# Context and weights laid out by the host with the contraction on partitions, and one tile for the last FFN chunk

## What is computed

```python
q = x @ Wq.T
k_raw = context @ Wk.T
v_raw = context @ Wv.T
kv = jnp.concatenate([k_raw, v_raw], axis=-1)
kv = kv.reshape(b, m, NHEADS, HEAD_DIM, 2)
q = _rmsnorm(q)
k = _rmsnorm(k)
scores = jnp.einsum('bhnd,bhmd->bhnm', q, k) * scale
attn = jax.nn.softmax(scores, axis=-1)
out = jnp.einsum('bhnm,bhmd->bhnd', attn, v)
W = (wq.astype(jnp.float32) - ZERO_POINT) * scale[:, None]
return jnp.einsum('bsd,hd->bsh', x, W)
...
gate = jax.nn.silu(gate)
return _qlinear(gate * up, wq_down, s_down)
...
x = x + jnp.tanh(g_xattn[0]) * _L0_xattn_ref(_layernorm(x, axis=-1), ctx_2048, L0_xattn_Wq, L0_xattn_Wk, L0_xattn_Wv)
x = x + jnp.tanh(g_ffn[0]) * _L0_ffn_ref(_layernorm(x, axis=-1), L0_ffn_wq_gate, L0_ffn_s_gate, L0_ffn_wq_up, L0_ffn_s_up, L0_ffn_wq_down, L0_ffn_s_down)
```

## Time and profile before

| what | us |
|---|---|
| three runs: median (lowest to highest) | 267.28 (266.71 to 267.42) |
| the profiled execution | 267.05 |
| its span in the profile | 265.2 |
| start of turn0 in iterations 2 to 5 | 107.66, 133.47, 159.28, 185.06 |
| one iteration of the loop | 25.8 |

### The profile page before, as it was taken

How to read it: one execution, slowest core, us unless ns; L and a number is a source line. 1 busy time by engine, 2 the same in 40 slices (tenths; PEclk the granted TensorE clock), 3 DMA queues, 4 the chain that set the end, 5 groups by cost and what they waited for, 6 DMA issues and landing times.

```text
span 265.2 us, 7329 instructions
## 1 busy us (share of the span) xinstructions
PE 219.6 (83%) x2592; PEld 178.5 (67%) x2592; DVE 176.5 (67%) x583; ACT 177.8 (67%) x338; POOL 106.3 (40%) x145
## 2 busy tenths in 40 slices
PE   1663979659879999899989989998999697965864
PEld 1553758437657878688777868786878585855764
DVE  4487999934665776687658765876596674657162
ACT  3258585844867895789578867885897667534250
POOL 5012212021322463645464455446444735434451
PEclk9999597956988999999999999999999999996799
DMA  5897522233075022603160406050506070000001
GB/s 178 216 352 178 62 56 49 54 45 62 0 101 101 0 56 49 136 3 72 26 138 0 87 12 138 0 100 3 121 0 82 13 109 2 21 22 0 20 20 40
DMA packets 45127, 18.08 MB, mean 68 GB/s; under 512 B 36400, under 2 KB 44848, under 8 KB 45104
## 3 DMA queue, kind: packets, MB, share of 16 engines
q1 hardware_dynamic: 45104, 17.77, 31.6%
HBM read 7.28 MB, written 2.10 MB: 35 GB/s over the span
## 4 chain that ended last, share of the span: by engine, by line
DVE 30%; PE 29%; issue 15%; POOL 14%; ACT 7%; DMA 2%; SPq 1%; DVEq 1%; POOLq 0%; ACTq 0%
PE bank L1278 7%; PE bank L1363 5%; POOL qk_parts L422 4%; POOL qk_unit L462 4%; PE pv_ps L1242 4%; POOL h_lo L430 4%; PE bank L1388 3%; DVE sums L899 3%; DVE hidden L990 3%; PE score_ps L1223 2%; PE bank L1311 2%; DVE silu L975 2%; DMA w_raw<-L_xattn_Wv_dram 2%; POOL x_all L439 2%; PE bank L1265 2%
## 5 line engine op out<-in xcount | busy, mean ns | idle before, releaser
L526 ACT ACTIVATE probs<-score_ps 128x1024 f32<-128x1024 f32 x64 | 65.9, 1032 | 3.5 <-PE score_ps L1223 3.5
L1363 PE MATMUL bank<-x_hi,gu_hi 128*128 128x256 f32 (+1 forms) x192 | 51.0, 301 | 4.7 <-DVE hidden L990 2.0
L462 POOL TENSOR_TENSOR qk_unit<-qk_raw,root_y 128x512 f32<-128x512 f32 x16 | 17.4, 1085 | 85.4 <-DVE root_y L783 85.4
L1363 PE MATMUL bank<-x_lo,gu_hi 128*128 128x256 f32 (+1 forms) x192 | 48.4, 286 | 0.0
L1242 PE MATMUL pv_ps<-probs,v_blocks 128*32 128x128 f32 x1024 | 42.8, 286 | 6.2 <-issue 4.2
L430 POOL TENSOR_TENSOR h_lo<-hidden,h_hi 128x256 fp32r<-128x256 f32 (+1 forms) x48 | 35.3, 745 | 24.8 <-ACT h_hi L651 24.4
L1363 PEld LDWEIGHTS bank<-x_hi,gu_hi 128*128 128x128 f32 (+1 forms) x192 | 35.3, 184 | 9.5 <-DVE hidden L990 2.4
L1363 PEld LDWEIGHTS bank<-x_lo,gu_hi 128*128 128x128 f32 (+1 forms) x192 | 35.5, 185 | 0.0
L1242 PEld LDWEIGHTS pv_ps<-probs,v_blocks 128*32 128x32 f32 x1024 | 24.9, 112 | 15.5 <-issue 7.4
L640 ACT ACTIVATE tanh_g<-bank,half_gate 128x256 f32<-128x256 f32 (+1 forms) x48 | 22.8, 475 | 18.2 <-PE bank L1363 16.0
L1278 PE MATMUL bank<-w_hi,xc_hi 128*128 128x256 f32 x96 | 31.7, 330 | 2.4 <-DVE xc_lo L889 2.4
(11 more groups left out here) (108 smaller groups left out, 435.2 us busy)
## 6 DMA issues: line engine op xcount, KB each, us to landing
ctx_sb<-ctx_dram SPq DMA_DIRECT2D x16, 128.0 KB, 2.6
out_dram<-x_all SPq DMA_DIRECT2D x16, 128.0 KB, 1.8
x_all<-x_dram SPq DMA_DIRECT2D x1, 1536.0 KB, 10.5
dn_int<-L_ffn_wq_down_dram SPq DMA_DIRECT2D x1, 704.0 KB, 6.7
gu_int<-L_ffn_wq_gate_dram SPq DMA_DIRECT2D x1, 640.0 KB, 4.6
gu_int<-L_ffn_wq_up_dram SPq DMA_DIRECT2D x1, 640.0 KB, 5.7
x_all<-x_dram SPq DMA_DIRECT2D x1, 384.0 KB, 5.1
w_raw<-L_xattn_Wq_dram SPq DMA_DIRECT2D x1, 256.0 KB, 2.7
```

The lines of the kernel that those rows point to most:

```text
L462: nc.gpsimd.tensor_tensor(qk_unit[:], qk_raw[:], root_y[:, 0:2 * H].unsqueeze(2).to_broadcast([P, 2 * H, HD]), ALU.mult).then_inc(unit_rea ...
L526: nc.scalar.activation(probs[:, t % 2, :], score_ps[t % 2][:].rearrange("p h n -> p (h n)"), ACT.Exp, scale=float(HD) ** 0.5 / UNIT ** 2). ...
L1363: last = nc.tensor.matmul(bank[k][0:r, a * TOK:(a + 1) * TOK], w[:, j, a, c, 0:r], xx[:, c, :], start=(n == 1), stop=(n == (4 if wide_weig ...
```

## The change

The host hands over ctx transposed, (tile, 128, 2, 128) with the contraction first; the three W matrices transposed, with their columns already in the order in which the kernel stores heads; the gate and up integers transposed in 6 chunks of 128 rows; and the down integers transposed. In the last gate/up chunk the 64 gate rows and the 64 up rows form one tile of 128; in the last down chunk the 64 rows stand twice.

The kernel loses all transposes of ctx, W and FFN weights, with `prep`. xc_hi and xc_lo are drained from the bank for x alone (128x256). ctx is split straight from SBUF: `context_hi` on ScalarE and `context_lo` on GpSimd. FFN weights are split from the integers by `upper_ffn` (ScalarE, three of 128x1536, p=-1) and `lower_ffn` (VectorE, three of 128x1536, p=0); `widest_weight` now looks for a lower part that is not zero. `normalize` and `normalize2` move from ScalarE to VectorE as one tensor_scalar each, and their offsets go. K is projected before Q. Chunk 5 has 4 matmuls for 8: the gate comes out on partitions 0 to 63, the up half on 64 to 127. h_hi(5) is written to rows 64 to 127 and h_lo(5) to rows 0 to 63 of the same tile, so that down needs 1 matmul there for 2. Four issues of small loads become one, five of FFN weights two.

```diff
+    columns = (order[:, None] * HD + np.arange(HD)).reshape(-1)
+    keys_values = np.concatenate([Wk, Wv])
+    w = np.stack([Wq[columns], keys_values[0::2][columns], keys_values[1::2]])
+    w_t = w.transpose(0, 2, 1).reshape(3, KC, P, D).transpose(0, 2, 1, 3)
+    ctx_t = ctx.transpose(0, 2, 1).reshape(B, KC, P, S).transpose(0, 2, 1, 3)
+    gate_up = np.zeros((NJ, 2, P, D), np.int32)
...
+        gate_up[NJ - 1, 0, a * LAST:(a + 1) * LAST] = w[full:]
...
+    gu_t = gate_up.reshape(NJ, 2, P, KC, P).transpose(4, 0, 1, 3, 2)
...
+    down[NJ - 1, :LAST] = down[NJ - 1, LAST:2 * LAST] = wq_down.T[full:]
...
+            sp.dma_start(ctx_sb[:, 0, :, :], ctx[0]).then_inc(ctx_loaded[0], 16)
+            for m in (1, 0, 2):
+                sp.dma_start(w_raw[:, m, :, :], w_qkv[m]).then_inc(w_loaded[m], 16)
...
-            full = (NJ - 1) * P
-            for k, s in enumerate((s_gate, s_up)):
-                with nc.allow_non_contiguous_dma(reason="704 scales, one to a partition"):
-                    sp.dma_start(scales[:, k, 0:NJ - 1], s[0:full].rearrange("(j p) -> p j", p=P)).then_inc(small_loaded, 16)
-                sp.dma_start(scales[0:LAST, k, NJ - 1:NJ], s[full:HID].rearrange("(p j) -> p j", j=1)).then_inc(small_loaded, 16)
-            for k, w in enumerate((wq_gate, wq_up)):
-                sp.dma_start(gu_int[:, k, 0:NJ - 1, :], w[0:full, :].rearrange("(j p) d -> p j d", p=P)).then_inc(ffn_w_loaded, 16)
-                sp.dma_start(gu_int[0:LAST, k, NJ - 1, :], w[full:HID, :]).then_inc(ffn_w_loaded, 16)
-            sp.dma_start(dn_int[:], wq_down.rearrange("(c p) h -> p c h", p=P)).then_inc(ffn_w_loaded, 16)
+            sp.dma_start(scales[:, 0:2, :], s_gu).then_inc(small_loaded, 16)
+            sp.dma_start(gu_int[:], w_gu).then_inc(ffn_w_loaded, 16)
+            sp.dma_start(dn_int[:], w_dn).then_inc(ffn_w_loaded, 16)
             sp.dma_start(x_all[:, 4:B, :], x[4:B].rearrange("b p d -> p b d")).then_inc(x_loaded[2], 16)
...
-                    sp.wait_ge(ctx_turned, b + 3)
-                    sp.dma_start(ctx_sb[:, e, :], dram_tile(ctx, b + 4)).then_inc(ctx_loaded[e], 16)
+                    sp.wait_ge(ctx_lo_ready, b + 3)
+                    sp.dma_start(ctx_sb[:, e, :, :], ctx[b + 4]).then_inc(ctx_loaded[e], 16)
...
+                of = hidden_rows(j)
+                lower = h_lo[:, j, :] if j < NJ - 1 else h_hi[0:LAST, j, :]
+                if j == NJ - 1:
+                    pool.wait_ge(h_lo_ready, n)
+                nc.gpsimd.tensor_tensor(lower, hidden[of, j % 3, :], h_hi[of, j, :].bitcast(F32),
                                         ALU.subtract).then_inc(h_lo_ready, 1)
+                if j == NJ - 1:
+                    pool.wait_ge(h_lo_ready, n + 1)
+
+            def context_lo(p, e):
+
+                b = 2 * p + e
+                if has_tile(p, b + 2):
+                    pool.wait_ge(ctx_hi_ready, b + 3)
+                    nc.gpsimd.tensor_tensor(xc_lo[:, e, KC:2 * KC, :], ctx_sb[:, e, :, :], xc_hi[:, e, KC:2 * KC, :].bitcast(F32),
+                                            ALU.subtract).then_inc(ctx_lo_ready, 1)
 
             def add_attention(p, e):
...
                 split_chunks(p - 1, 1, (0, 1))
+                context_lo(p, 1)
                 qk_norm(p, 0)
                 split_chunks(p, 2, (2,))
                 split_qk(p, 0)
                 split_chunks(p, 2, (3, 4, 5))
                 add_attention(p, 1)
+                context_lo(p + 1, 0)
                 qk_norm(p, 1)
                 split_qk(p, 1)
-                if real(p, "y0"):
+                if here(p, "y0"):
...
+            def upper_ffn(part):
 
 ...
+                act.wait_ge(ffn_w_loaded, 16 * 2)
+                nc.scalar.activation(ffn_part(part, gu_hi, dn_hi), ffn_part(part, gu_int, dn_int), ACT.Identity,
+                                     bias=minus_zero_point[:]).then_inc(ffn_hi_ready, 1)
...
+                    nc.scalar.copy(xc_hi[:, e, 0:KC, :].rearrange("p a n -> p (a n)"), bank[k][:, 0:D]).then_inc(xc_hi_ready, 1)
+
+            def context_hi(p, e):
+
+                b = 2 * p + e
+                if has_tile(p, b + 2):
+                    act.wait_ge(ctx_loaded[e], 16 * (p + 2))
+                    if since(b, 0):
+                        k, m = use(p, "v0") if e else use(p - 1, "v1")
+                        act.wait_ge(filled[k], m)
+                    nc.scalar.copy(xc_hi[:, e, KC:2 * KC, :], ctx_sb[:, e, :, :]).then_inc(ctx_hi_ready, 1)
...
                 drain_v(p, 0)
-                if not first:
-                    normalize(p, 0)
+                context_hi(p, 1)
...
                 exp_octet(p, 1, 1)
                 if not ending(p):
                     upper(p, 2, 3)
-                    normalize2(p, 0)
                 upper(p, 2, 4)
                 drain_v(p, 1)
+                context_hi(p + 1, 0)
                 upper(p, 2, 5)
                 if first:
-                    convert_gate_up()
+                    upper_ffn(0)
                     square(p, 1)
                     copy_qk(p, 1)
-                    convert_down()
-                    normalize(p, 1)
+                    upper_ffn(1)
+                    upper_ffn(2)
                 else:
-                    normalize(p, 1)
                     square(p, 1)
                     copy_qk(p, 1)
...
+                nc.vector.tensor_scalar(xn[:, 1 - e, :], tile_of(b), x_mean_var[:, one, 0], x_root[1][:, one],
+                                        ALU.subtract, ALU.mult).then_inc(xn_ready, 1)
...
+            def normalize2(p, e):
+
+                b = 2 * p + e - 1
...
+                dve.wait_ge(root_steps, (ROOT_STEPS + 1) * (b + 4))
+                if since(b, 2):
+                    k, m = use(p if e else p - 1, "turn2")
+                    dve.wait_ge(filled[k], m)
+                nc.vector.tensor_scalar(x1n[:, 1 - e, :], tile_of(b), x1_mean_var[:, 0:1], root_y[:, 2 * H:],
+                                        ALU.subtract, ALU.mult).then_inc(x1n_ready, 1)
...
+                of = hidden_rows(j)
+                half = slice(TOK, 2 * TOK) if j < NJ - 1 else slice(0, TOK)
+                nc.vector.scalar_tensor_tensor(out=hidden[of, j % 3, :], in0=silu2[of, j % 2, :], scalar=scales[of, 2, j:j + 1],
+                                               in1=bank[k][of, half], op0=ALU.mult, op1=ALU.mult).then_inc(drained[k], 1)
...
+            def lower_ffn(part):
+
+                dve.wait_ge(ffn_hi_ready, part + 1)
+                nc.vector.scalar_tensor_tensor(out=ffn_part(part, gu_lo, dn_lo), in0=ffn_part(part, gu_int, dn_int), scalar=-ZERO_POINT,
+                                               in1=ffn_part(part, gu_hi, dn_hi).bitcast(F32), op0=ALU.add,
+                                               op1=ALU.subtract).then_inc(ffn_lo_ready, 1)
...
+                dve.wait_ge(ffn_lo_ready, part + 1)
+                lower = ffn_part(part, gu_lo, dn_lo).bitcast(F32)
+                nc.vector.tensor_reduce(weight_max[:, part:part + 1], lower, AX.XYZW if part < 2 else AX.XY, ALU.max,
+                                        apply_absolute_value=True).then_inc(w_max_steps, 1)
...
-                nc.vector.tensor_scalar(wide[:], wide_max[:], F32R_INTEGERS, None, ALU.is_gt).then_inc(w_max_steps, 1)
+                nc.vector.tensor_scalar(wide[:], wide_max[:], 0.0, None, ALU.is_gt).then_inc(w_max_steps, 1)
...
-                    widest_weight(0)
...
                 statistics2(p, 0)
+                normalize(p, 0)
...
-                        widest_weight(1)
-                        widest_weight(2)
+                        lower_ffn(0)
+                        lower_ffn(1)
+                        lower_ffn(2)
+                        widest_weight(0)
                     statistics2(p, 1)
                     sum_squares(p, 1)
 
                     root_inputs(p, 1)
                     roots(p, 1, 1, 1 if early else 4)
                 turn2_lo(p)
-                prep_y(p, 0)
                 if early:
                     roots(p, 1, 2, 4)
                 if second:
-                    any_wide_weight()
+                    widest_weight(1)
+                    widest_weight(2)
                 roots(p, 1, 5, 7)
-                x1_offset(p, 1)
+                normalize2(p, 1)
+                normalize(p, 1)
                 if first:
                     x_statistics(2, 4, 7)
 
+                qk_upper(p, 1)
                 if second:
-                    prep_y(p, 1)
-                qk_upper(p, 1)
+                    any_wide_weight()
                 if first:
                     x_statistics(2, 7, 10)
                 gate(p, 1, 0)
...
-                pe.wait_ge(ctx_loaded[e], 16 * (p + 2))
-                for c in range(KC):
-                    last = nc.tensor.transpose(bank[k][:, (KC + c) * P:(KC + c + 1) * P], ctx_sb[:, e, c * P:(c + 1) * P], ident[:])
-                last.then_inc(ctx_turned, 1)
...
```

(14 more changed lines are left out.)

355 lines of the change are left out of this document (104 added, 251 removed).

## The result

| | median us (lowest to highest, runs) |
|---|---|
| kernel before | 267.35 (266.71 to 271.48, 4) |
| changed kernel | 286.26 (285.28 to 288.34, 4) |
| ratio | 1.073, 95% interval 1.065 to 1.081 |
| predicted | 273.7, range 266 to 280 |

The profiled execution of the changed kernel took 285.28 us, its span is 283.5. The direction was forecast, the size was not: +18.3 us of span where +6.6 stood. The changed kernel itself was timed on the first chip alone, so the ratios of its variants are to be held against its 1.073, and a gain of 1 us or less is read from stages of the traces only.

A forecast was written before the change was run, and what follows sets the result against it. No single engine bounds it; TensorE's gap before turn0 hangs on a line through VectorE and GpSimd. From 267.05: gate +5.7, p=1 -.5, five pairs +2.5, end -1.1 give 273.7 us, range 266 to 280.

The forecast's parts named there:

- what TensorE is spared: Steady state: context transposes .5, down .6, chunk 5 .5, together 1.6 us a pair on an engine with 24.5.
- the gate: p=0, VectorE's work from out_divide to wide's end: 15.5 to 16 us against 7.45, net +5.7, bounds +2 to +7.5.
- the 4.20 us: p=0: TensorE's idle time, read as standing until the branch on `wide` is decided.
- the -.5: p=1: TensorE at half clock is the bound, and two pairs of transposes less save .5 us.
- Half e=0: Steady state, first half of a pair: -.27 + .6 - .3 = 0, no gain; bounds -.6 to +.5.
- the term that decides: Half e=0: normalize2 on VectorE held until GpSimd's qk_unit ends, +.6 us, with hidden(3) and the cast behind it.
- Half e=1: Steady state, second half of a pair: sum +.5 us a pair, over five pairs +2.5.
- -.2 for h_hi(5): Half e=1, ScalarE: x1n (.61) leaves and context_hi (.41) comes, so h_hi(5) comes .2 us earlier.
- The +.4 behind step 7: Half e=1, VectorE behind root step 7: normalize held until qk_unit's end, the cast .25 later, together +.4 us.
- rival 1: Clock falls behind TensorE's gap of about 2.5 us: 1.2 a time in three of five pairs, +3.6, 277.3; chance .2.
- The end: Pair 7's FFN alone: chunk 5 -.5 and down -.6, together -1.1 us.
- The rule named ahead: VectorE, chunk 5: output starting in another 32-partition group waits until earlier ones end; some .3 us a pair worse.

The follow-up runs named there:

- e6_pe_back: Changed kernel with TensorE's work given back unused (chunk 5, each turn's transposes, first matmul of each down half done twice): 287.97 us, ratio 1.077.
- g1_late_branch: Changed kernel with TensorE's branch on wide taken in iteration 1, just ahead of chunks 0 and 1, instead of ahead of iteration 1: 281.65 us, ratio 1.046.
- b1_norm_dve: Kernel before with only normalize and normalize2 moved to VectorE as tensor_scalar, without the offsets: 272.50 us, beside 271.02 of the kernel before on that chip.
- f1_hhi_first: Changed kernel with ScalarE's h_hi(5) ahead of v1's drain and of context_hi, iterations -1 to 9: 281.55 us, ratio 1.055.
- f4_all_fill: f3_all with 8 unused transposes in TensorE's gap before turn0: 267.74 us, ratio 1.003.
- f3_all: Changed kernel with the wide test on upper parts (lower_ffn behind it), early load of ctx[2], and h_hi(5) ahead of v1's drain: 273.38 us, ratio 1.025.

## Why the prediction was right or wrong

**Right**: the side, that no single engine binds and that what TensorE is spared is worth next to nothing by itself (e6_pe_back; it is 1.0 to 1.3 us a pair and not 1.6); that the gate grows by VectorE's work and that ctx[2] holds ScalarE (6.37 us).

**The gate, +5.7 for +7.1**: mechanism right in the main, the stretch too short. It was 17.1 and not 15.5 to 16, since two lower_ffn met GpSimd (2.27 for 1.75) and x1n did too (1.26 for .34). The first exp gained nothing instead of .5 (ctx[2] at 21.73, not 20.8), but out_divide came 2.5 earlier for the 2.7 of the sum. The upper bound, 7.5, held it. One reading was wrong and cost the sum nothing: the 4.20 us were put down to the decision on `wide`, and g1_late_branch shows that they belong to the branch. At iteration 1 the -.5 became +.1.

**Half e=0**: x1n held, .9 longer where I took +.6. The sum of this half, 0, was no worse for it, but "the term that decides" decided nothing: b1_norm_dve shows the same hold at an unchanged period.

**Half e=1, the step that failed in the loop**: "-.2 for h_hi(5)". I set x1n's departure from ScalarE against context_hi's arrival as if ScalarE were busy there. It idles .99 for v1, so what leaves ahead of that wait gives nothing, and what comes behind it is paid in full: h_hi(5) +.65, the addition +.95 where I had +.1. Two of the additions (context_hi, GpSimd's wait for its own end) stood exactly there. The +.4 behind step 7 came out at +.1 (addition to turn0 9.83 for 9.76): VectorE had idled 1.24 us for qk_unit there, and the two normalisations fill that. The period is +1.0 to +1.2 for +.5.

**The clock, the largest error**: the sum put it at nothing; rival 1 came true and had .2. The earlier trace rows showed gaps of 2.31 with the clock left at 1.00 and of 2.94 with it gone, and I took the value between as a border. There is none so simple: 2.26 did nothing in iteration 3 and was followed by .89 in iteration 4; 1.33 to 1.7 were followed by .94 in b1_norm_dve and f1_hhi_first, and 1.02 was in f4_all_fill. It costs 1.3 to 1.5 us where the stage's mean is .94 and 2.3 where it is .89, for 1.2 in my price, and it falls in every iteration from 4 on, not in three of five. In iterations 4 and 5 it is 3.5 us.

**The end, -1.1 for +3.3** (with iteration 6, -.6 for +3.3): I took the spared matmuls off the time as if TensorE were the bound there. It waits for VectorE's hidden, and longer than before (3.13 us for 2.31 at out0, 3.60 for 2.94 at x1n's transposes), and the mean clock is .87 for .96. The fill of f4_all_fill brought it from 83.1 (f3_all) to 81.1, so 2 us of it are the clock's by an experiment; the rest, up to the 79.9 of before, I didn't separate.

Of the 11.7 us missed in the span, roughly: gate, start and iteration 1 2, the period at full clock 2.4, the clock in iterations 4 and 5 3.5, the end 3.9.

The rule named ahead (the Trainium skill, "VectorE: DVE Perf Modes", "Two Vector instructions with no wait between them") now has its rows: VectorE of the changed kernel around chunk 5, whose silu and hidden begin at partition 64 (timeline).

```profile
128.24 0.48 DVE L955 SCALAR_TENSOR_TENSOR hidden<-silu,scales,bank 128x256 f32<-128x256 f32 x1
128.75 0.41 DVE L939 SCALAR_TENSOR_TENSOR silu<-tanh_g,bank 64x256 f32<-64x256 f32 x1
129.20 0.49 DVE L955 SCALAR_TENSOR_TENSOR hidden<-silu,scales,bank 64x256 f32<-64x256 f32 x1
129.72 0.43 DVE L856 TENSOR_TENSOR xc_lo<-bank,xc_hi 128x256 fp32r<-128x256 f32 x1
```

The instructions follow each other at .51, .45 and .52; in the kernel before the same three distances (119.42 to 120.66) are .40, .44 and .40. That is .24 us a pair, near the .3 that I had by the page; the trace agrees with it.

## What to carry to other kernels

In a queue that runs in order, look for the idle time in front of each instruction that you add or remove: work taken away ahead of such a wait is worth nothing, work added behind it costs its full time, and an instruction whose input is early belongs ahead of the wait (h_hi(5): some 4 to 5 us by one line). Follow an added wait through every queue that it stands in: ctx[2] held ScalarE, and once that was cured, GpSimd. On TensorE a longer line elsewhere and fewer matmuls both lengthen the gap (1.15 before, 1.67 with the line as short as before in f1_hhi_first, 2.26 in the changed kernel), and gaps can be paid a second time by the clock: here a kernel with more matmuls was 5.6 us faster. And before you move a branch to hide the wait for its condition, look whether the wait is for the condition at all.

## What the hardware did that I had not expected

- VectorE and GpSimd on SBUF hold or stretch one another in both directions: GpSimd's 128x256 subtraction took 2.23 us for .72 beside lower_ffn, which took 2.27 for 1.75; a 128x256 scalar_tensor_tensor with both operands in SBUF was held like a tensor_scalar (1.31 and 1.14), and when VectorE came .06 first, qk_unit took 1.36 for 1.07.
- The clock falls behind gaps of 1.0 to 2.4 us in some iterations of one and the same loop and not in others.
- TensorE's branch costs 4.1 to 4.4 us of idle time even where its condition was ready 16 us earlier (g1_late_branch).
